# Scattering eight token batches in two slots of an attention's drain in place of four

## What is computed

```python
x = x + attention_L0(layernorm(x), ctx)      # 16 heads of 8 columns: the "dense" attention L0x
x = x + experts_L0(layernorm(x))             # L0m: each token goes to 1 of 8 experts, argmax of the router
x = x + attention_L1(layernorm(x), ctx)      # L1x: 16 heads of 64 columns
x = x + ffn_L1(layernorm(x))                 # L1f
x = x + two_attentions_and_ffns_L2(layernorm(x), ctx)   # L2a1, L2f1, L2a2, L2f2
x = x + experts_L2(layernorm(x))             # L2m: 2 of 8 experts a token
x = x + attention_L3(layernorm(x), ctx)      # L3x: 16 heads of 8 columns, dense again
x = x + experts_L3(layernorm(x))             # L3m: 1 of 8 experts a token
```

## Time and profile before

| what | us |
|---|---|
| median of 3 runs | 1390.44 |
| lowest and highest of them | 1384.25, 1392.7 |
| the profiled execution's own time | 1382.45 |
| its span | 1380.7 |

### The profile page before, as it was taken

How to read it: one execution, slowest core, us unless ns; L and a number is a source line. 1 busy time by engine, 2 the same in 40 slices (tenths; PEclk the granted TensorE clock), 3 DMA queues, 4 the chain that set the end, 5 groups by cost and what they waited for, 6 DMA issues and landing times.

```text
span 1380.7 us, 37780 instructions
## 1 busy us (share of the span) xinstructions
PE 1019.2 (74%) x15068; PEld 757.8 (55%) x15068; DVE 899.1 (65%) x2420; ACT 727.2 (53%) x1479; POOL 611.2 (44%) x575
## 2 busy tenths in 40 slices
PE   3788478889898565788977578978379675776774
PEld 2455366556677343356764356756267553555664
DVE  4677454788777995888975577866344266766432
ACT  5776355776555434555436456666155364664321
POOL 2566633354354432454551355642611345657132
PEclk9788588999999776788978779989589785887787
DMA  3321321110010101100001000000221112110122
GB/s 95 92 84 43 92 58 53 61 33 25 17 34 10 37 17 35 36 3 10 4 3 38 1 2 3 4 2 4 89 75 34 51 34 67 40 31 28 55 74 69
DMA packets 59721, 53.24 MB, mean 39 GB/s; under 512 B 10590, under 2 KB 47966, under 8 KB 59358
## 3 DMA queue, kind: packets, MB, share of 16 engines
q1 hardware_dynamic: 53777, 41.62, 10.4%
q0 software_dynamic: 4096, 8.40, 2.0%
q10 hardware_dynamic: 1679, 0.81, 0.2%
HBM read 33.90 MB, written 16.25 MB: 36 GB/s over the span
## 4 chain that ended last, share of the span: by engine, by line
PE 35%; issue 27%; DVE 23%; ACT 8%; POOL 3%; DMA 2%; POOLq 0%; ACTq 0%; SPq 0%; DVEq 0%
PE psum L671 12%; PE psum L1174 7%; PE psum L1192 6%; DVE area L1831 4%; PE psum L794 2%; PE psum L834 2%; DVE stats L1812 2%; ACT area L1261 2%; DVE area L1974 1%; DVE area L1988 1%; ACT xn L1285 1%; POOL sorted_in L2746 1%; DVE negm L1967 1%; DVE area L2127 1%; PE psum L678 1%
## 5 line engine op out<-in xcount | busy, mean ns | idle before, releaser
L1261 ACT ACTIVATE area<-psum 128x512 bf16<-128x512 f32 (+4 forms) x278 | 144.8, 540 | 206.1 <-PE psum L834 133.4
L1831 DVE TENSOR_TENSOR area<-psum,area 128x512 bf16<-128x512 f32 (+3 forms) x270 | 159.7, 620 | 50.4 <-ACT area L1261 46.8
L2472 DVE TENSOR_TENSOR area<-area 128x512 bf16<-128x512 f32 x106 | 73.4, 695 | 146.3 <-ACT area L1729 93.4
L2616 POOL TENSOR_TENSOR area<-area 77x1024 bf16<-77x1024 f32 x64 | 120.0, 1891 | 73.6 <-ACT area L1435 73.6
L1192 PE MATMUL psum<-moe,area 128*128 x1272 | 111.1, 229 | 24.2 <-issue 23.3
L1174 PE MATMUL psum<-xT_hi,moe 128*128 128x128 bf16 x848 | 115.5, 238 | 17.0 <-issue 13.7
L2572 POOL TENSOR_TENSOR moe<-stage,moe 128x512 bf16<-128x512 f32 x47 | 54.9, 1168 | 126.0 <-ACT moe L1256 126.0
L1435 ACT ACTIVATE area<-psum 77x1024 f32<-77x1024 f32 (+1 forms) x96 | 92.8, 1017 | 28.9 <-PE psum L794 28.9
L1192 PEld LDWEIGHTS psum<-moe,area 128*128 128x128 bf16 x1272 | 86.7, 102 | 37.5 <-issue 27.7
L2624 POOL TENSOR_SCALAR_AFFINE_SELECT area<-area 128x1024 bf16<-128x1024 bf16 x64 | 72.3, 1149 | 68.4 <-DVE area L1974 57.4
L1174 PE MATMUL psum<-xT_lo,moe 128*128 128x128 bf16 x424 | 95.3, 237 | 8.6 <-issue 8.5
(11 more groups left out here) (246 smaller groups left out, 3009.0 us busy)
## 6 DMA issues: line engine op xcount, KB each, us to landing
area<-sorted_in SPq DMA_DIRECT2D x22, 256.0 KB, 3.6
sorted_out<-area SPq DMA_DIRECT2D x22, 256.0 KB
stage<-in_w_L0m SPq DMA_DIRECT2D x16, 256.0 KB
stage<-in_w_L2m SPq DMA_DIRECT2D x16, 256.0 KB
stage<-in_w_L3m SPq DMA_DIRECT2D x16, 256.0 KB
sorted_in<-area SPq DMA_DIRECT2D x2, 1472.0 KB, 7.3
stage<-in_w_L2a SPq DMA_DIRECT2D x8, 320.0 KB
stage<-in_w_L1x SPq DMA_DIRECT2D x6, 320.0 KB
```

What stands on the lines that cost most here:

```text
L1261: ins = act.activation(out, bank, ACT.Copy)
L1831: ins = dve.tensor_tensor(out, bank, high, ALU.subtract)
L2472: dve.tensor_tensor(R.HL[u], R.HF[u], upper(R.HF[u]), ALU.subtract).then_inc(K.tile_split, tiles.one())
L2616: pool.tensor_tensor(A.PL[n % 4][0:A.L], A.PF[n % 4][0:A.L, :].rearrange("p (h q) -> p h q", h=8), A.PH[n % 4][0:A.L], ALU.subtract).then_ ...
```

## The change

The attention gets a table from step to batches, `scattered_at`, and the loop looks the step up in it. Three scatters now stand in step 16 (batches 0 to 2) and five in step 17 (batches 3 to 7); steps 18 and 19 have none. Both dense attentions use the table. All else stays: the order within a step, the second half's scatters, the loads and the splits.

```diff
--- before.py
+++ after.py
@@ -460,7 +460,7 @@
     def __init__(self, K, name, number, order, residual, bq=None, bk=None, bv=None, bo=None, late=None):
         self.name, self.number, self.order, self.residual, self.late = name, number, order, residual, late
 
-        self.then = None
+        self.then, self.scattered_at = None, {16: range(3), 17: range(3, HB)}
 
         self.begun = 2 if late is not None else 1
         self.bq, self.bk, self.bv, self.bo = bq, bk, bv, bo
@@ -2689,8 +2689,8 @@
             if 0 <= b - 2 < B:
                 exponentials_lo(b - 2, 0)
                 exponentials_lo(b - 2, 1)
-            if 16 <= b < 20:
-                scatter(A.then, 0, range(2 * (b - 16), 2 * (b - 16) + 2))
+            if b in A.scattered_at:
+                scatter(A.then, 0, A.scattered_at[b])
             for n in K.loads_of(A.name, b):
                 split_weights(n)
         rstd(slice(0, 128), group(3))
```

## The result

| | us |
|---|---|
| before, median of 20 runs | 1387.51 (1383.1 to 1392.7) |
| changed, median of 20 runs | 1392.7 (1388.87 to 1399.61) |
| ratio, with its 95% interval | 1.0044 (1.0028 to 1.006) |

The ratio less one, times 1387.51, is 6.1 us, its interval 3.9 to 8.3; the medians differ by 5.2. The forecast was +3.8 us and 1394. It started from 1390.44, the median of the three runs then shown; over 20 runs the kernel before stands 2.9 lower. The change is under the 1% bound, as forecast.

A forecast was written before the change was run, and what follows sets the result against it. It took GpSimd to set the pace in both drains, with the gate starting the routed stage; 2.9 (L0x) plus 0.9 (L3x) gave 3.8 us, so 1390.4 + 3.8 = 1394, range 1385 to 1399.

The forecast's parts named there:

- The gate starts the stage, not the tiles: At L0m's start: the wait for four engines' drains starts the routed stage; tiles have 0.8 to 0.9 us to spare.
- L0x's term: First drain: the gate moves from 166.34 to 169.3, +2.9 us, through the later load of chunk 21.
- exponentials 15: Low halves of batch 15's exponentials on GpSimd; in the first drain they start at 151.45 instead of 150.15.
- split 19: GpSimd's weight split of chunk 19 in the first drain: ends at 161.6 instead of 156.50, 5.1 us later.
- load of chunk 21: First drain: SP's load waits for split 19 to free its buffer; ScalarE's copy begins 3.31 us after that split ends.
- the third rival: First drain: chunk 21's load suffers from tile loads behind it, 1.2 to 4.8 us more, 1395.4 to 1399; 10%.
- The cover in L0x: First drain: group 3's later moments cost nothing, covered by the later wait for chunk 21, up to 167.1.
- comparison of expert numbers: VectorE, first drain: held by two splits until 163.0, it would make the moments 2.6 us late, still 1.2 ahead.
- L3x's term: Second drain: later exponentials 15 delay group 3's moments by 1.28 us and the gate by +0.9, between 0 and +1.3.
- clock rival: TensorE's longer pause before L0m delays its clock rise, costing up to 1.5 us more: 1395.7; 5%.
- the fourth rival: The clock rival: matmuls at half speed after L0m's gate, up to 1.5 us more; 5%.
- 2% on each side: Whole-kernel chance left on each side of no change, for a shift that no row shows.

The follow-up runs named there:

- experiment 5: Changed kernel with all eight scatters in step 16, in both attentions; 1.0129 of the kernel before, +17.3 us.
- 1: Changed kernel with the table of three and five in L0x alone, L3x keeping two scatters a step; 1.0034 of the kernel before, +4.7 us.
- 4: Changed kernel with one scatter in step 16 and seven in step 17, in both attentions; 1.0035 of the kernel before, +4.9 us.
- 10: The changed kernel measured again, on another chip; 1.004 of the kernel before, +5.4 us.
- experiment 7: Changed kernel with the chunk's split ahead of the five scatters in step 17 alone; 1.0016 of the kernel before, +2.2 us.
- 9: The table filled with two scatters in each of steps 16 to 19, the instructions of the kernel before; 1.0002 of it, +0.3 us.
- 2: Changed kernel with the table of three and five in L3x alone, L0x keeping two scatters a step; 1.0025 of the kernel before, +3.5 us.
- 3: Changed kernel with the chunk's split ahead of the scatters in every step; 1.0031 of the kernel before, +4.3 us.
- 6: Kernel before with the two scatters of step 16 moved ahead of group 2's reciprocal deviation on GpSimd; 1.0016 of the kernel before, +2.2 us.
- 8: Kernel before with the first scatter alone moved ahead of group 2's reciprocal deviation on GpSimd; 0.9978 of the kernel before, -3.0 us.

## Why the prediction was right, and which term was too small

- **The gate starts the stage, not the tiles.** Shown: in the changed kernel the tile loads are issued 2.1 us earlier from the indices (22.29 against 24.38) and TensorE starts 3.3 later; in experiment 5 tile loads issued as early as that (22.31) go with a start 6.2 later. From the gate TensorE starts after 2.10 and 1.74 us, before 2.03 and 1.74. That this is the reading of registers was argued, not shown.
- **L0x's term, 2.9 forecast, 3.3 measured.** Every step came as written: exponentials 15, the last scatter and split 19 (161.6) within 0.1 us. The load of chunk 21 took 3.65 us in the chain, 3.67 from the split's end to the copy, where I had 3.31: that is the 0.3. It was 3.6 to 3.7 again in experiments 1, 4 and 10, where the copy stands at 25.53 to 25.58. If the last scatter took the 2.24 us of before, it had just landed (164.59 + 2.24), and the four tile loads were issued from 0.4 us behind the chunk. In experiment 7, with scatters beside it and no tile loads, it was 3.56 (161.46 to the copy at 145.92 + 19.10). What sets it between 3.3 and 3.7 was not tried. The crowded transfer of the third rival, 1.2 us or more, did not come.
- **The cover in L0x.** The late moments cost nothing while chunk 21 was later still: they ended 25.80 + 0.38 behind the indices and rstd 3 began at 27.76. The comparison of expert numbers took 3.31 us there, from 165.08 to the end of the two splits, and the moments came 2.58 late (2.6 forecast). In experiment 7, where no split lies over it, it took 0.19. The turn-taking that the page "SBUF — State Buffer" of the Trainium skill describes under "Who interferes with whom" fits the length of the wait, and the trace adds that VectorE did not get in between two of GpSimd's instructions issued back to back. It does not fit the order as the rows have it: the comparison's row begins 0.49 us before the first of the two splits (165.08 and 165.57; before, 158.42 and 158.95), while GpSimd is still at a scatter, and alone it would have been over in 0.19. My reading in the prediction passed over that; why it was held is open.
- **L3x's term, 0.9 forecast, 1.8 measured.** This is the term that was mis-sized. The step "exponentials 15 end 1.28 later, and ... the moments of group 3 hang on them one after another" was right, but it passed the delay on at 1.28; it arrived as 2.24. 0.81 of the rest is the eight logit matmuls at the lower clock (1.82 against 1.01). The last 0.15 is no more than two kernels of the same order differ by: in experiments 1 and 9, whose L3x has the order of before, the moments began at 18.31 and 18.30 behind the indices, before at 18.15. Every kernel with three or more scatters ahead of exponentials 15 shows 1.82 in L3x (changed, 2, 3, 5, 7, 10), every one with at most two shows 1.01 (before, 1, 4, 6, 8, 9). I had named a clock rival, but placed it behind the gate of L0m and at 5%, and the sum put the clock in the drain at nothing. That the stall keeps the clock down is how the rows of L3x stand together; the clock by itself was not varied. L0x gives no such rule. There the logits took 1.88 us before, in 2, 8 and 9 without any stall of the output matmuls, and 1.06 in 4, with a stall of 0.30, and in 6. In the changed kernel the ten output matmuls ahead of a stall of 2.12 us took 0.49 us, the ten behind it 0.80; in experiment 10, the same kernel, they took 0.81 ahead of it too. So the logits of L0x met the lower clock with the stall and without, and the change could lose nothing at them.
- **Nothing is seen to be given back later.** From the gate of L0m to the write of the second half's row indices it was 25.58 us before and 25.58 with the change, and 25.4 to 25.95 in the ten others. The clock rose at the same place behind the gate as well: in four stretches of 3 us from the gate on it was 0.50, 0.50, 0.50 and 0.98 before, 0.50, 0.50, 0.51 and 1.00 with the change, so the fourth rival did not come. Further on only the whole time speaks. The time's differences agree with the sums of the gates in the changed kernel and all ten others within their intervals. Ten of the eleven lie 0.3 to 3 us on the slow side of their sums, though; kernels measured together share the runs of before, and whether anything stands behind it is left open.
- **Base.** That 1394 lies only 1.3 above the measured 1392.7 is in part luck: the shift was 1.3 too small by the gates, the base 2.9 too high, and the two errors work against each other. The chances of the cases add up to 100%, so the 2% on each side that the prediction also sets aside have no room in them.

## What to carry to other kernels

Work moved earlier on an in-order engine pushes something later, and if that is a subtraction that frees a staging buffer, a transfer time is added behind it: here eight equal transfers issued earlier made the stage later, and one split put ahead of the last five took L0x's 3.3 us back. Look for the last signal into a barrier before making the data behind it earlier. To gain, put such work into the engine's idle time and only as much as fits: of a gap of 4.2 us only 2.4 lay behind the indices; one scatter in it paid, two delayed the chain behind it.

## What the runs showed of the hardware that was not expected

- A stall of 0.89 us of TensorE in the drain of L3x goes with a granted clock that stays at 0.50 for the next 5 us, where it was 0.78 without the stall. In L0x the clock was at 0.50 at that place without a stall too.
- A VectorE operation of 0.19 us was held for 3.31 us until the end of two GpSimd subtractions in a row, though its row begins 0.49 us before the first; where only indirect transfers ran on GpSimd it was not held.
- The same drain repeats within 0.05 us on chips whose times for the whole kernel differ by 3% (1387.6 and 1344.5).
